# Attentions three and four fed one sequence at a time, key stacks in two loads, and a reordered set-up in an eight-stage transformer kernel

## What is computed

```python
x = x + _L0_xattn_ref(_layernorm(x), ctx, ctx_lens, ...)   # a0: 8 heads of 16
x = x + _L0_ffn_ref(_layernorm(x), ...)                    # f0: shared + top 2 of 8 experts, gelu
x = x + _L1_xattn_ref(_layernorm(x), ctx, ctx, mask, ...)  # a1: 8 heads of 128, relative positions
x = x + _L1_ffn_ref(_layernorm(x), ...)                    # f1: inner layer + top 2 of 8, silu
x = x + _L2_xattn_ref(_layernorm(x), ctx, ctx, mask, ...)  # a2: 16 heads of 8
x = x + _L2_ffn_ref(_layernorm(x), ...)                    # f2: top 2 of 8, relu
x = x + _L3_xattn_ref(_layernorm(x), ctx, ctx, ...)        # a3: 16 heads of 8, biases
x = x + _L3_ffn_ref(_layernorm(x), ...)                    # f3: top 1 of 8, gelu
```

## Time and profile before

| | us |
|---|---|
| median of three runs (778.00 to 779.56) | 779.11 |
| the profiled execution | 783.57 |
| its span, first to last instruction | 781.8 |
| mean granted clock of TensorE, share of full | 0.904 |
| TensorE busy, matmul / weight load | 640.2 / 493.5 |
| VectorE / ScalarE / GpSimd busy | 412.6 / 374.5 / 185.7 |

### The profile page before, as it was taken

One profiled execution on the slowest core, in us unless ns is written; L12 is line 12 of the kernel. 1 busy time (PEld: TensorE's weight loads), 2 busy tenths in 40 slices (PEclk: granted clock), 3 DMA queues, 4 the chain that ended last, 5 costly groups with the idle time before them and its releaser, 6 DMA issues.

```text
span 781.8 us, 14348 instructions
## 1 busy us (share of the span) xinstructions
PE 640.2 (82%) x4788; PEld 493.5 (63%) x4788; DVE 412.6 (53%) x1417; ACT 374.5 (48%) x935; POOL 185.7 (24%) x356
## 2 busy tenths in 40 slices
PE   3498679998998997778798699987996767977890
PEld 2165579885655665577697356756996534545890
DVE  5774542523265578755526756752443666774220
ACT  7065235554464545946355246551332145655560
POOL 1224421030040011411430611141313231221211
PEclk9599679999999999979989879996998869999996
DMA  7795099010788774010394132323173403431211
GB/s 222 193 333 203 21 177 200 27 28 28 154 240 237 194 232 99 28 52 23 106 213 121 40 81 70 108 79 77 56 216 75 117 21 85 159 101 49 78 51 50
DMA packets 98482, 90.76 MB, mean 116 GB/s; under 512 B 11204, under 2 KB 89669, under 8 KB 98316
## 3 DMA queue, kind: packets, MB, share of 16 engines
q1 hardware_dynamic: 94828, 82.51, 39.9%
q0 software_dynamic: 3584, 7.35, 3.6%
HBM read 53.06 MB, written 35.59 MB: 113 GB/s over the span
## 4 chain that ended last, share of the span: by engine, by line
PE 53%; DVE 14%; POOL 9%; DMA 8%; issue 8%; ACT 5%; SPq 0%; POOLq 0%; DVEq 0%; ACTq 0%
PE bank L1919 12%; PE bank L1940 10%; PE bank L1758 3%; PE bank L1706 3%; PE bank L1741 3%; PE bank L2050 2%; POOL rows_sorted L657 2%; PE bank L2017 2%; PE bank L1854 2%; PE bank L1896 2%; POOL xm L667 2%; PE bank L1879 2%; DVE negmax L914 2%; PE bank L1614 1%; POOL rstd L632 1%
## 5 line engine op out<-in xcount | busy, mean ns | idle before, releaser
L1940 PE MATMUL bank<-W,spare 128*128 128x128 f32 (+1 forms) x960 | 133.3, 284 | 2.3 <-ACT spare L1502 2.1
L1940 PEld LDWEIGHTS bank<-W,spare 128*128 128x128 f32 x960 | 123.0, 200 | 4.1 <-issue 2.7
L914 DVE TENSOR_REDUCE negmax<-bank 128x2 f32<-128x512 f32 x128 | 85.1, 688 | 32.7 <-PE bank L1706 26.1
L1418 ACT ACTIVATE late<-bank 128x512 f32<-128x512 f32 x120 | 70.7, 594 | 54.0 <-PE bank L1746 25.5
L1706 PE MATMUL bank<-big 128*128 128x256 bf16 x320 | 71.5, 300 | 18.8 <-DVE negmax L914 17.4
L1502 ACT ACTIVATE spare<-bank,W 128x128 f32<-128x128 f32 x224 | 63.6, 370 | 41.0 <-PE bank L1919 41.0
L657 POOL DMA_INDIRECT rows_sorted<-xn,idx x56 | 55.8, 997 | 105.7 <-DVE idx L991 91.1
L1741 PE MATMUL bank<-big 128*128 128x256 bf16 x320 | 75.6, 287 | 4.7 <-DMA big<-nmT 3.3
L1706 PEld LDWEIGHTS bank<-big 128*128 128x128 bf16 x320 | 28.3, 104 | 46.4 <-DVE negmax L914 28.7
L1550 ACT ACTIVATE big<-big,r 128x256 f32<-128x256 f32 x64 | 31.9, 500 | 47.8 <-DVE r L1240 46.9
L1758 PE MATMUL bank<-late 128*32 128x256 f32 x480 | 43.9, 396 | 0.1
(11 more groups left out here) (280 smaller groups left out, 1348.6 us busy)
## 6 DMA issues: line engine op xcount, KB each, us to landing
W<-in_f_wx SPq DMA_DIRECT2D x25, 578.0 KB, 7.1
late<-bands_scratch SPq DMA_DIRECT2D x8, 1024.0 KB, 5.8
W<-in_f_wx SPq DMA_DIRECT2D x8, 514.0 KB, 3.6
big<-parts_scratch SPq DMA_DIRECT2D x4, 768.0 KB, 7.0
bands_scratch<-zrow SPq DMA_DIRECT2D x4, 768.0 KB, 13.9
stage<-rows_sorted SPq DMA_DIRECT2D x11, 256.0 KB, 3.9
rows_sorted<-stage SPq DMA_DIRECT2D x11, 256.0 KB, 4.0
bands_scratch<-late SPq DMA_DIRECT2D x3, 764.0 KB, 6.0
```

What stands on the lines that cost most here:

```text
L914: ins = v.tensor_reduce(negmax[:, g % 2, :, j], bank[i % 2][:, :].rearrange("p (t k) -> p t k", t=2), AX.X, ALU.max, negate=True)
L1418: a.activation(PTs[j % NPT][:, :, :], bank[2 + j % 2][:, :].rearrange("p (c q) -> p c q", c=2), ACT.Exp)\
L1940: ins = mm(dst[:, 128 * place_:128 * (place_ + 1)], hidB[n % 3][:, c, :], w2[:, 128 * c:128 * (c + 1)], start=c == 0, stop=c == FC - 1)
```

## The change

1. Attentions three and four take queries by sequence: four pieces of two tiles instead of pieces of two, two and four. Pieces 2 and 3 are combined, normed, turned, projected, split and stacked on their own, at steps 14 to 19 and 21 to 26 (`LATER`), and stacked at groups 4 and 6.
2. The key stack of a2 and a3 is still written at once but read in two loads of 512 columns; the second goes after `y_out` of quad 1 of half 1. The scores wait for it at sequence 2.
3. On GpSimd maxima 0 go ahead of the first gathers; of the four tiles' gathers two come after the norm of piece 1 and two after that of piece 2.
4. `rows_in("f1", 1)` goes ahead of `y_out("f1", 0, 3)`.
5. Set-up: one constant block ahead of the first keys, the other and the zeroing of the values behind the second keys; half 0 of x turned (in another bank) and projected between the two key products; SP waits for the first query stack before it writes the second keys. `wide_tables` goes behind the norm of the first mixture's half 0.

```diff
-SECOND_HALF = {"a2": 15, "a3": 15}
+LATER = {2: 14, 3: 21}
...
+            if side:
+                return sem("st.wk"), 48 * (hf + 1 if n == 0 else n + 2)
+            return sem("st.wq"), 48 * (hf + 1 if n == 0 else 4 * n + hf - 1)
...
-            return 7 if name in ("f1.0", "f1n.0") else M[usual]
+            return {"f1.0": 7, "f1n.0": 7, "a0.0": PVB[1]}.get(name, M[usual])
...
+            if side:
+                cols = slice(512 * half, 512 * (half + 1))
...
             stack_in("a0", 0, 0)
-            stack_out("a0", 1, 1)
             sp.wait_ge(sem("c.maskrow"), 1)
...
+            sp.wait_ge(*landed("a0", 0))
+            stack_out("a0", 1, 1)
             stack_out("a0", 0, 1)
...
+            rows_in("f1", 1)
             y_out("f1", 0, 3)
-            rows_in("f1", 1)
             stack_out("a2", 1)
             own_in()
-            stack_in("a2", 1)
+            stack_in("a2", 1, 0)
...
+                stack_in(key, 1, 1)
                 stack(key, 0, 0)
                 y_out(before, 1, 2)
-                stack_out(key, 0, "h")
+                stack_out(key, 0, 1)
                 y_out(before, 1, 3)
-                stack_in(key, 0, "h")
+                stack_in(key, 0, 1)
...
-                    if g == 4:
-                        stack_out(key, 0, 1)
+                    if g in (4, 6):
+                        stack_out(key, 0, g // 2)
                     maxima_to_rows(key, g)
-                    if g == 4:
-                        stack_in(key, 0, 1)
+                    if g in (4, 6):
+                        stack_in(key, 0, g // 2)
...
+                if name == "f0.0":
                     wide_tables()
-                if name in ("a2.h", "a3.h"):
-                    for t in range(4):
-                        fetch_results(BEFORE[name[:2]], 1, [t])
-                        if t < 3:
-                            maxima_parts(name[:2], [t])
                 if name in ("a2.1", "a3.1"):
-                    maxima_parts(name[:2], range(3, 13))
+                    maxima_parts(name[:2], [0])
+                    fetch_results(BEFORE[name[:2]], 1, [0])
+                    maxima_parts(name[:2], [1])
+                    fetch_results(BEFORE[name[:2]], 1, [1])
+                    maxima_parts(name[:2], [2])
+                if name in ("a2.2", "a3.2"):
+                    fetch_results(BEFORE[name[:2]], 1, [2])
+                    maxima_parts(name[:2], [3])
+                    fetch_results(BEFORE[name[:2]], 1, [3])
+                    maxima_parts(name[:2], [4])
+                if name in ("a2.3", "a3.3"):
+                    maxima_parts(name[:2], range(5, 13))
...
+                    for hf, start in LATER.items() if late_half else ():
+                        if i == start - 4 and hf == 2:
+                            weights(BEFORE[key], 1)
+                        if i == start:
+                            combine(BEFORE[key], 1, (2 * hf - 4, 2 * hf - 3))
+                            if hf == 3:
+                                x_ready(dve, key, 1)
+                            norm_stats(key, hf, x)
+                        if i == start + 1:
+                            norm_apply(key, hf, x, xn)
+                        if i == start + 5:
+                            query_parts(key, hf)
...
-                    project(key)
+                    project(key, (0,))
                     copy_T(key, 0, nT[0])
                     queries(key, 0)
...
+                    project(key, (1,))
+                    fill(big[96:128, 8192:12288], zrow[96:128, :], "c.rows")
+                    fill(late[:, 0:4096], zrow[:, :], "c.Va")
...
-                    keys(key)
+                    keys(key, (0,))
                     turn_norm(key, 0)
                     queries(key, 0)
+                    keys(key, (1,))
                     values(key)
```

More of the change, by code:

```diff
@@ L400, in stack_out @@
                     sp.dma_start(scratch[side, first:first + n, :, cols].rearrange("r p t -> p r t"), src)\
-                      .then_inc(*written(side, half))
+                      .then_inc(written(key, side, half)[0], 16)
             def stack_in(key, side, half=None):
@@ L409, in stack_in @@
                     sp.wait_ge(sem("c.zero"), 16)
-                sp.wait_ge(written(side, half)[0], 48 * writes(key, side, half))
+                sp.wait_ge(*written(key, side, half))
                 src = scratch[side].rearrange("r (i h) t -> (r i) h t", h=H)
@@ L413, in stack_in @@
                     sp.dma_start(dst[row:row + (r1 - r0) * d, 0:H, cols], src[r0 * d:r1 * d, :, cols])\
[L414 removed]
+                      .then_inc(sem(f"st.k{half}") if side else landed(key, half)[0], 16)
             def stack(key, side, half=None):
@@ L776, in query_parts @@
                     return
-                dve.wait_ge(written(1, None)[0], 48 * writes(key, 1, None))
+                dve.wait_ge(*written(key, 1, 1))
                 split(QT, piece(key, hf), "qp")
@@ L1349, in queries @@
                 scale = NARROW[key][2]
-                act.wait_ge(*at(key, "q", place_of(key, hf)))
+                act.wait_ge(*at(key, "q", hf + 1))
                 cols = piece(key, hf)
-                qt, src = QT[:, cols], bank[M[int(hf != 1)]][:, 0:cols.stop - cols.start]
+                qt, src = QT[:, cols], bank[M[int(key != "a0" and hf < 2 or hf == 0)]][:, 0:cols.stop - cols.start]
                 if key == "a3":
@@ L1641, in _, with keys @@
             pe.wait_ge(sem("ld.qk"), 16)
-            def keys(key):
+            def keys(key, halves_=(0, 1)):
                 w = 4 * LAYER_OF[key]
-                for c in range(2):
+                for c in halves_:
                     if key == "a0":
@@ L1806, in attention @@
                         out_project(b - 1)
-                    if key != "a0" and i == SECOND_HALF[key] + 3:
-                        turn_norm(key, 1)
-                        queries(key, 1)
+                    for hf, start in LATER.items() if key != "a0" else ():
+                        if i == start + 3:
+                            turn_norm(key, hf)
+                            queries(key, hf)
                     if key == "a2" and i == 2:
```

111 lines of the change are left out of this document (45 added, 66 removed).

## The result

| | before | after |
|---|---|---|
| median of four runs, us | 779.3 | 752.3 (749.2 to 754.7) |
| ratio | | 0.965, 95% interval 0.960 to 0.970 |
| profiled execution's span, us | 781.8 | 746.8 |
| mean granted clock of TensorE | 0.904 | 0.937 |

The prediction was 749 us with a range of 742 to 760.

The account below looks back on a forecast made before the run. TensorE's work plus its stops, each paid as wait and slower clock, was taken to bound the kernel. Six gains summing to 33.7 us, less charges, gave 30.2 off 783.6: 753.4, scaled to 749 us, range 742 to 760.

Parts of the forecast that it names:

- set-up: Start of kernel: clearing one constant block before the first keys moves VectorE's chain to the first maximum forward, 1.4 us.
- wide tables: First mixture: GpSimd builds them behind the norm, in its hole before the first scatter; TensorE gains its wait, 1.9 us.
- second mixture: seam, less gathers: Half 1's rows loaded before quad 3's store save a 4.4 us wait and slow clock: 7.0 us, less 1 for gathers.
- third mixture: key load: Halved key load before attention four lets gathers land earlier: 5.4 us wait plus 2.4 clock, 7.8, less 0.5 for shorter runs.
- attention three: Maxima ahead of gathers and pieces by sequence bring step 26 to 458.1 from 465.25: 7.2 us, less 1 for clock.
- attention four: Same count gives 6.2 us to step 26, plus a later 2.88 us stop mostly gone: 8.4, less 1 for clock.
- queries read at 11.2: Set-up: bank of half 0's queries free at 11.2, so VectorE splits the second keys at 14.0 instead of 15.44.
- the gathers of half 0 start where they did. They are next: Second mixture, behind the seam: gathers keep their start and become the next limit; 1 us charged against the halved key load.
- Rival (e): Orders don't bind: the rows' scatter lands only near 385, or new waits hold SP; seam gives nothing, 756 us; chance 0.07.
- rival (b): Third mixture: gathers aren't freed, being slow by themselves or by y_out; 7.8 us lost, 757 us; chance 0.10.
- Rival (a): Attentions three and four: longer chain returns half of 15.6 us as waits at steps 18 and 24; 757 us; chance 0.16.
- Rival (d): Many short waits in steps 6 to 32 keep the clock at 1.2 GHz through the steady part; 785 us; chance 0.03.

Follow-up runs that it names:

- one key load: Changed kernel with the key stack of attentions three and four read in one load of all 1024 columns again: 763.1 us, ratio 0.979 to the kernel before.
- experiments 9 to 12: Changed kernel again (0.967); with fitted dummy products and second mixture's first key load behind a store (0.969); those plus set-up dummies (0.964); that load's place alone (0.970).
- the disturbed one: Changed kernel with dummy products where TensorE waits around the third and fourth mixtures; profiled execution spans 758.6 us; measured 749.8 us, ratio 0.965.
- gathers first: Changed kernel with the gathers of tiles 4 and 5 ahead of maxima 0 and 1 again, in attentions three and four: 757.4 us, ratio 0.973.
- experiments 1 and 2: First: kernel before, second mixture's half 1 rows loaded ahead of quad 3's store, 783.0 us, 1.004. Second: changed kernel, whole key load again, 763.1 us, 0.979.
- old set-up: Changed kernel with both constant blocks first, keys of both halves, then half 0 of x; wide tables stay moved: 754.0 us, ratio 0.968.
- seam undone: Changed kernel with the store of quad 3 ahead of half 1's rows again in the second mixture: 752.9 us, ratio 0.971.

## Why the prediction was right, and where it wasn't

The total was right by terms that were partly wrong: the set-up and the two mixtures gave 4.8 us less than forecast and the two attentions 4.3 more. That these nearly cancel is luck. Against the stages, using all profiles that share a stage's code:

| term | forecast | measured | from |
|---|---|---|---|
| set-up | 1.4 | 0.1 | 67.54 less 67.41 |
| wide tables | 1.9 | 2.0 | 35.2 less 33.2 |
| second mixture: seam, less gathers | 6.0 | 4.7 | 90.0 less 85.3 |
| third mixture: key load | 7.3 | 5.1 | 20.9 less 15.8 |
| attention three | 6.2 | 8.4 | 114.8 less 106.4 |
| attention four | 7.4 | 9.5 | 104.8 less 95.3 |
| sum | 30.2 | 29.8 | |

Each side is the mean over the profiles of the ledger that have the code in question. The medians differ by 27.0; the 2.8 us between lie within what single stages scatter.

**Set-up: the step that failed** is "queries read at 11.2", and after it "VectorE splits the second keys at 14.0". TensorE and ScalarE in the changed kernel:

```profile
8.07 0.60 ACT L1391 ACTIVATE QKT<-bank 128x512 f32<-128x512 f32 x1 [2.38 <-PE bank L1662]
9.58 2.07 PE L1638 MATMUL bank<-nT,aw 128*128 128x512 f32 x2 [0.69 <-ACT nT L1357]
12.43 2.05 PE L1662 MATMUL bank<-cT,aw 128*128 128x512 f32 x2 [0.78 <-ACT QKT L1367]
14.51 0.60 ACT L1391 ACTIVATE QKT<-bank 128x512 f32<-128x512 f32 x1 [2.23 <-PE bank L1662]
```

The product of the queries starts 1.8 us earlier than before, as counted, and the second keys' product waits for the bank as counted. But the copy of the queries that frees it ends at 12.29, not 11.2: at the lower clock their product takes 2.07 us, for which the kernel before, at 11.39, had needed 1.13. With another 2.05 us for the keys VectorE's split comes at 15.14 against 15.44: 0.3 of the 1.4 us. In the second profile of the same kernel, though, TensorE and VectorE show:

```profile
9.59 1.13 PE L1638 MATMUL bank<-nT,aw 128*128 128x512 f32 x2 [0.69 <-ACT nT L1357]
13.64 0.42 DVE L821 CAST big<-QKT 128x512 bf16<-128x512 f32 x1
```

Here the product runs at the full clock and the split comes 1.8 us earlier than before. The profiles with the new order fall into these two kinds. With a product of 1.12 or 1.13 us (one key load, and the four of experiments 9 to 12) maxima 7 come at 65.8 to 66.3 us, 1.3 to 1.8 under the mean of the old order. With 2.07 us (the other four of the ledger, and the disturbed one) they come at 67.3 to 68.1, and nothing is gained. With the old order the product starts at 11.2 to 11.6 us and took 1.12 or 1.13 in all four. So the order is worth the forecast 1.4 us when the clock is up by 9.6 us and nothing when it isn't. The same kernel shows both, and so do two of these kernels on one chip (one key load, gathers first), so which one comes isn't set by the edit; why it differs stays open. The prediction took the duration from one execution.

**Wide tables.** VectorE's wait for the power fell from 4.00 us to 1.48. But the clearing and the selects that now run right behind it slow VectorE:

```profile
71.39 2.56 DVE L778 TENSOR_SCALAR xn<-x_res,mv,rstd 128x128 f32<-128x128 f32 x4 [1.48 <-POOL rstd L635]
72.77 5.00 POOL L678 TENSOR_SCALAR_AFFINE_SELECT late<-late 128x1024 bf16<-128x1024 bf16 x4
74.10 1.02 DVE L893 TENSOR_TENSOR rc<-rc,qmask 128x8 f32<-128x8 f32 x1
76.75 1.31 DVE L977 TENSOR_TENSOR xm<-lg 128x256 f32<-128x256 f32 x1
```

The normalising took 1.11 us in the earlier trace rows and takes 2.56 here; a product of eight columns takes 1.02 us, which takes 0.17 at 79.78 without a neighbour. "They lie in GpSimd's hole" costed the cover at nothing; it costs about 3 us of VectorE's time in the three lines shown, and 2.0 us of TensorE's are gained all the same. The Trainium skill (SBUF — State Buffer, Who interferes with whom) says that the two engines share a port pair that one of them holds for a whole instruction; the lengthened instructions here agree, though no run was made on it.

**Second mixture.** The step "the gathers of half 0 start where they did. They are next" is right to name them, and its price of 1 us is the failure. I took the load out of their way by half, and didn't see that the seam itself puts the load ahead of them: I moved the rows' load past the store and left the instructions behind it on SP (written keys, own rows, key load) where they had been. With the whole load the term is a loss of 2.5 us (experiments 1 and 2). Rival (e), "the seam gives nothing", named another cause: the load did not go late, and SP was not held. The sentence that in the second mixture "the gathers were landed when wanted" was true of the kernel before only, because TensorE's 4.38 us stop had delayed SP.

**Third mixture.** The mechanism was the one named, and rival (b) is out: with the load whole, the gain is gone. TensorE's wait fell from 5.91 to 1.68 us, 4.2 of the 5.4; VectorE still waits 1.20 us for tile 1's gathers (570.38), which were issued at 565.06 and 566.31, behind a half load issued from 560.04 on. The clock behind it is 1.00 in this profile, as said. Over the four profiles with either load, the part up to the norm of tiles 0 and 1 gives 4.2 us (5.4 counted) and the part behind it 0.9 (2.4 counted): two of the four with the half load (old set-up, seam undone) still take 8.6 and 8.7 us there, with 3.4 us at the lower clock, about as much as with the whole one. So the clock's share of this term was taken from one execution too.

**Attentions three and four.** The count by hand gave 7.2 us to step 26 of attention three; from the norm of tiles 2 and 3 to step 26 it is 46.91 us before and 39.54 after, 7.4. (The count has a slip: 12.9 us from 445.6 end at 458.5, not 458.1.) Some 0.8 us more are gained behind step 26, which the count left out, and no run says why. The sum then took off 1 us for each attention for a clock kept low by short stops; in attention three the clock was 1.00 throughout, so that charge was 1 us too much. In attention four the mean clock is 0.79 as before, and the gain is there all the same: from the norm of tiles 2 and 3 to maxima 7 TensorE stood five times over 1.3 us before (2.65, 3.21, 1.55, 1.47 and 2.88), after only once (1.72). In the mean over the profiles 5.6 us are gained up to step 26 (6.2 counted) and 3.9 behind it, where the count had 2.2; that second part, and the 1 us charged for the clock, were mis-sized. Rival (a) put maxima 3 and the later pieces on a chain that would bring half of it back: no wait over 1.72 us is left. Rival (d), the slower clock through the steady part, didn't come: 1.00 over the 41 us that end attention three.

**Chance.** The prediction read its clock terms from one execution. Of the 8 us between the profiled gain and the medians', 4.5 are that start, where before drew the long slow stretch; the rest is spread (the changed kernel's profile has the lowest second mixture of three, 83.7 against 86.1).

## What to carry to other kernels

Moving an instruction forward in a queue moves all that stands behind it; write down what each of them will now be ahead of on the other queues, bulk loads above all. Of two edits one may be worth little and the other less than nothing (1.6 and -2.5 us here), and both together 4 to 6 us, so a single edit that fails isn't yet a reason to drop the idea. And when two profiles are compared, cut both at the same instructions and find the stages whose code hasn't changed: what differs there is the size of the chance. A duration that depends on the clock should be read from several executions before it goes into a sum.

## What the runs showed of the hardware

A gather issued 0.53 us behind a load of 0.75 MB on another queue served its reader only when the load was over (its second part took 9.1 us); one issued 2 us ahead of it had landed after 2.5 us. The same stop of 1.35 to 1.40 us was followed by 17 us of the lower clock in one execution and by 7 in another. The first product of the queries, 9.6 us into the same kernel, took 2.07 us in one execution and 1.13 in another. A VectorE product of eight columns took 1.02 us beside GpSimd's selects on 1024 columns and 0.17 without them.
